# A three-step software pipeline on one core: fewer waits on TensorE and a new hand-written order of the second stage

## What is computed

```python
for i in range(DEPTH):                                   # DEPTH = 6, on x of (8, 512, 128)
    x = attn_layer(shift_tokens(x), Wqkv[i], q_scale[i], k_scale[i], Wo[i]) + x
    x = ffn_layer(shift_tokens(x), ln_g[i], ln_b[i], W1[i], b1[i], W2[i], b2[i]) + x

def attn_layer(x, Wqkv, qs, ksc, Wo):
    q, k, v = jnp.split(x @ Wqkv, 3, -1)                 # 16 heads of 64
    q, k = l2norm(q) * qs, l2norm(k) * ksc
    q = q * cos * scale + rotate_half(q) * sin * scale
    k = k * cos * inv + rotate_half(k) * sin * inv
    return local_attention(q, k, v) @ Wo                 # windows of 32, each sees itself and the one before

def ffn_layer(x, g, bln, W1, b1, W2, b2):
    xn = (x - mu) / jnp.sqrt(var + 1e-05) * g + bln
    a, gate = jnp.split(xn @ W1 + b1, 2, -1)             # 341 wide each
    return a * gelu(gate) @ W2 + b2
```

## Time and profile before

| What | Value |
|---|---|
| Median of 3 runs | 4945.61 us (4935.18 to 4952.09) |
| The profiled execution, its own time | 4938.53 us |
| Its span, first to last instruction | 4936.4 us |
| PE busy | 4103.4 us (83%), 60260 matmul records |
| DVE busy | 4056.8 us (82%) |
| POOL busy | 3516.9 us (71%) |
| ACT busy | 2979.7 us (60%) |
| Mean granted TensorE clock | 0.853 of full |

### The profile page before, as it was taken

The page is one execution under the profiler, slowest core; times in us unless marked ns, Lnnn a source line. Parts: engine busy times, 40 slices in busy tenths (PEclk is TensorE's granted clock), DMA queues, the critical chain, the costliest instruction groups (busy, mean ns, idle before and its releaser), DMA issues. The chain is left out here.

```text
span 4936.4 us, 154683 instructions
## 1 busy us (share of the span) xinstructions
PE 4103.4 (83%) x60260; PEld 2147.1 (43%) x60260; DVE 4056.8 (82%) x7132; ACT 2979.7 (60%) x4240; POOL 3516.9 (71%) x1655
## 2 busy tenths in 40 slices
PE   3666666666647999899999999899998999899995
PEld 1233223233223555455544555455554555455552
DVE  6999999999956888788878888788887888788883
ACT  5999999999953555445544555455544555455441
POOL 4999999999965676666766676567665766576661
PEclk9755555555558999999999999999999999999997
DMA  0000000000004444444553444444444444444443
GB/s 14 3 5 9 5 9 5 5 9 5 7 8 107 114 113 109 113 103 109 116 123 92 107 113 109 99 114 111 109 114 97 113 109 109 98 118 109 108 98 82
DMA packets 234267, 382.36 MB, mean 77 GB/s; under 512 B 38432, under 2 KB 63776, under 8 KB 233504
## 3 DMA queue, kind: packets, MB, share of 16 engines
q1 hardware_dynamic: 229408, 371.06, 31.9%
q10 hardware_dynamic: 4224, 2.10, 0.1%
HBM read 51.89 MB, written 18.87 MB: 14 GB/s over the span
## 5 line engine op out<-in xcount | busy, mean ns | idle before, releaser
L734 POOL TENSOR_TENSOR W<-W 128x1280 f32<-128x1280 f32 x416 | 954.9, 2319 | 141.2 <-ACT W L585 139.9
L585 ACT ACTIVATE W<-S,lam 128x512 f32<-128x512 f32 (+3 forms) x2048 | 952.0, 553 | 84.2 <-DVE lam L878 72.9
L1702 POOL TENSOR_TENSOR m<-m 128x1024 f32<-128x1024 f32 x384 | 902.6, 2362 | 68.3 <-DVE m L1810 68.2
L849 DVE BATCH_NORM_STATS2 stats<-W 128x6 f32<-128x512 f32 (+3 forms) x2048 | 832.4, 478 | 57.6 <-POOL W L734 56.5
L1708 POOL TENSOR_TENSOR sm<-sm,mx 128x1024 f32<-128x1024 f32 x192 | 451.7, 2353 | 504.7 <-DVE mx L1824 504.7
L1319 PE MATMUL pb<-xs,wg 128*128 128x512 f32 x1536 | 760.4, 630 | 52.8 <-DMA xs<-hist 38.4
L1555 ACT ACTIVATE lnn<-pb,cst 128x1024 f32<-128x1024 f32 x192 | 213.9, 1114 | 806.7 <-PE pb L1326 806.7
L1833 DVE SCALAR_TENSOR_TENSOR nf<-rn,m 128x1024 f32<-128x1024 f32 x384 | 616.7, 1637 | 93.0 <-ACT rn L1564 77.7
L1550 ACT ACTIVATE sq<-pb 128x1024 f32<-128x1024 f32 x384 | 381.9, 1021 | 491.8 <-PE pb L1319 491.8
L1698 POOL TENSOR_TENSOR sqs<-sq 128x1024 f32<-128x1024 f32 x192 | 456.9, 2379 | 225.2 <-ACT sq L1550 225.2
L1713 POOL TENSOR_TENSOR pr<-pr,rsum 128x1024 f32<-128x1024 f32 x192 | 407.4, 2122 | 292.6 <-DVE rsum L1846 290.3
(11 more groups left out here) (120 smaller groups left out, 7124.4 us busy)
## 6 DMA issues: line engine op xcount, KB each, us to landing
qkn<-nf SPq DMA_DIRECT2D x1536, 128.0 KB, 2.4
vr<-v SPq DMA_DIRECT2D x96, 768.0 KB, 5.9
vr<-v SPq DMA_DIRECT2D x96, 192.0 KB, 5.5
xr<-hist SPq DMA_DIRECT2D x48, 256.0 KB, 2.9
hist<-xo SPq DMA_DIRECT2D x48, 256.0 KB, 3.8
wg<-wqkv SPq DMA_DIRECT2D x24, 384.0 KB, 3.8
xs<-hist SPq DMA_DIRECT2D x48, 128.0 KB
vr<-v SPq DMA_DIRECT2D x96, 64.0 KB, 6.2
```

The costliest lines, as they stand in the source:

```text
L585: ins = nc.scalar.activation(W[:, p, h, c], S[:, j % 2, h, c], ACT.Abs_reciprocal_sqrt, bias=lam[:, j, i:i + 1])
L734: nc.gpsimd.tensor_tensor(W[:, p, h, :], W[:, p, h, :], W[:, p, h, :], ALU.mult).then_inc(s_wp[p], 1)
L849: ins = nc.vector.bn_stats(out=stats[:, p, h * NBLK + u, :], in_=W[:, p, h, UOFF[u]:UOFF[u] + UNIT[u]])
L1702: nc.gpsimd.tensor_tensor(m1[:, which, :, :], m1[:, which, :, :], m2[:, which, ::-1, :], ALU.add)\
```

## The change

Nothing is computed in another way. Four things differ, all in `stage2`.

1. PE's waits for inputs move out of the task functions into small functions (`weights_due` and so on), which `body` calls right ahead of the task. Waits that repeat one already passed are gone: `weights_due` stands once per group (4 and not 12 waits per step), `inputs_due` once (not twice), `normed_due` once (2 and not 8). PE's body has 35 waits for inputs where it had 50. The waits of `take` stay, with other partners.
2. PE's order and the banks in `HOLD` are new. `q3` and `k3` move from the end of body b to the start of body b + 1 (lag 1). `up1` stands ahead of `k0` and `q0`, `k0` ahead of `q0`, `weigh0` ahead of `v3`, `var` behind `turn0`, `out` ahead of both halves of `score0`, and `up0` between the halves of `weigh2`.
3. The orders of ACT, POOL, DVE and SP are new. On POOL `normalise(b, 0)` moves from the start of body b + 1 to the end of body b, behind both `add_rotated(b, 2, ...)`. On ACT `squares(b, 2, 1)` stands ahead of `squares(b, 2, 0)`, and `values(b, 2)` ahead of `inverse_norms(b, 2)`. On DVE `rotate(b, 3, 1)` comes ahead of `rotate(b, 3, 0)`, behind `scale`. On SP `load_xs` comes ahead of the second `load_projections`, and `store` takes step b - 2.
4. Three bodies are unrolled ahead of the loops, not four. DVE's `residual` gets one more wait (`s_xo` of the step before).

```diff
         HOLD = [
-            ("var", 2, 3), ("turn0", 1, 0), ("v3", 1, 2), ("weigh0", 1, 4), ("norm3", 1, 0), ("gate1", 2, 7),
-            ("gate0", 2, 2), ("score2", 1, 4), ("q0", 0, 0), ("k0", 0, 4), ("up1", 2, 3), ("turn1", 1, 6),
-            ("v0", 0, 2), ("weigh1", 1, 6), ("norm0", 0, 4), ("k1", 0, 0), ("q1", 0, 4), ("score3", 1, 6),
-            ("v1", 0, 2), ("turn2", 1, 6), ("up0", 2, 2), ("weigh2", 1, 6), ("norm1", 0, 0), ("score0", 0, 2),
-            ("out", 2, 6), ("turn3", 1, 4), ("q2", 0, 0), ("weigh3", 1, 4), ("k2", 0, 6), ("wo", 1, 3),
-            ("score1", 0, 0), ("norm2", 0, 6), ("mean", 1, 3), ("q3", 0, 4), ("v2", 0, 2), ("k3", 0, 6),
+            ("turn0", 1, 2), ("var", 2, 0), ("q3", 1, 6), ("k3", 1, 0), ("weigh0", 1, 2), ("v3", 1, 4),
+            ("norm3", 1, 0), ("gate0", 2, 6), ("gate1", 2, 3), ("score2", 1, 0), ("up1", 2, 2), ("k0", 0, 4),
+            ("q0", 0, 0), ("turn1", 1, 6), ("v0", 0, 2), ("weigh1", 1, 6), ("k1", 0, 0), ("norm0", 0, 4),
+            ("score3", 1, 2), ("v1", 0, 6), ("turn2", 1, 2), ("q1", 0, 4), ("weigh2", 1, 2), ("up0", 2, 6),
+            ("norm1", 0, 6), ("out", 2, 0), ("score0", 0, 4), ("turn3", 1, 2), ("q2", 0, 6), ("weigh3", 1, 2),
+            ("k2", 0, 0), ("wo", 1, 5), ("score1", 0, 6), ("norm2", 0, 0), ("mean", 1, 3), ("v2", 0, 4),
         ]
...
+            def due(s, value):
+                pe.wait_ge(s, value)
+                pe.sem_inc(held["pe"], 1)
+
+            def weights_due(n, g):
+                due(wg_in[g], 16 * n + 16)
+
+            def inputs_due(n):
+                due(xs_in, 32 * n + 32)
...
             def project(n, g, which, out):
-                pe.wait_ge(wg_in[g], 16 * n + 16)
-                pe.sem_inc(held["pe"], 1)
-                if g == 0:
-                    pe.wait_ge(xs_in, 32 * n + 32)
-                    pe.sem_inc(held["pe"], 1)
...
@@ PE, body(b)
+                if live(b, 2):
+                    take("up1", b)
+                    ups(b - 2, 1, bank("up1"))
+                if live(b, 0):
+                    take("k0", b)
+                    weights_due(b, 0)
+                    inputs_due(b)
+                    project(b, 0, 1, bank("k0"))
+                if live(b, 0):
+                    take("q0", b)
+                    project(b, 0, 0, bank("q0"))
...
@@ ACT, body(b)
                 if live(b, 0):
+                    squares(b, 2, 1)
+                if live(b, 0):
                     squares(b, 2, 0)
                 if live(b, 0):
-                    squares(b, 2, 1)
...
@@ POOL, end of body(b)
                 if live(b, 0):
+                    square_sums(b, 2)
+                if live(b, 0):
+                    add_rotated(b, 2, 1)
+                if live(b, 0):
                     add_rotated(b, 2, 0)
                 if live(b, 0):
-                    square_sums(b, 2)
+                    normalise(b, 0)
...
@@ DVE, residual and body(b)
             def residual(n):
+                dve.wait_ge(s_xo, at(n - 1, 0, 1))
+                dve.sem_inc(held["dve"], 1)
...
+                if live(b, 1):
+                    scale(b - 1)
+                if live(b, 0):
+                    rotate(b, 3, 1)
                 if live(b, 0):
                     rotate(b, 3, 0)
-                if live(b, 1):
-                    scale(b - 1)
-                if live(b, 0):
-                    rotate(b, 3, 1)
+                if live(b, 0):
+                    weighted(b, 0)
...
```

More of the change, by code:

```diff
@@ L1286, in _ @@
                     body(l * BATCH + k, l, k)
-            for b in range(STEPS, STEPS + 3):
+            for b in range(STEPS, STEPS + 2):
                 body(b, DEPTH, b - STEPS)
@@ L1455, in body @@
                 if live(b, 1):
-                    norms(b - 1, 3, take("norm3", b))
+                    take("v3", b)
+                    values(b - 1, 3, bank("v3"))
+                if live(b, 1):
+                    take("norm3", b)
+                    squares_due(b - 1, 3)
+                    norms(b - 1, 3, bank("norm3"))
                 if live(b, 2):
-                    gates(b - 2, 1, take("gate1", b))
+                    take("gate0", b)
+                    normed_due(b - 2)
+                    gates(b - 2, 0, bank("gate0"))
@@ L1473, in body @@
+                    probabilities_due(b - 1, 1)
+                    turn(b - 1, 1, bank("turn1"))
                 if live(b, 0):
-                    values(b, 0, take("v0", b))
+                    take("v0", b)
+                    weights_due(b, 1)
+                    values(b, 0, bank("v0"))
                 if live(b, 1):
-                    weigh(b - 1, 1, 0, take("weigh1", b))
+                    take("weigh1", b)
+                    turned_due(b - 1, 1)
+                    weigh(b - 1, 1, 0, bank("weigh1"))
@@ L1499, in body @@
                 if live(b, 0):
-                    norms(b, 1, take("norm1", b))
+                    take("norm1", b)
+                    squares_due(b, 1)
+                    norms(b, 1, bank("norm1"))
+                if live(b, 2):
+                    take("out", b)
+                    gated_due(b - 2)
+                    ffn_out(b - 2, bank("out"))
                 if live(b, 0):
-                    scores(b, 0, 0, take("score0", b))
-                if live(b, 2):
-                    ffn_out(b - 2, take("out", b))
+                    take("score0", b)
+                    rotated_due(b, 0)
+                    scores(b, 0, 0, bank("score0"))
                 if live(b, 0):
@@ L1507, in body @@
                 if live(b, 1):
[L1508 removed]
+                    take("turn3", b)
+                    probabilities_due(b - 1, 3)
+                    turn(b - 1, 3, bank("turn3"))
                 if live(b, 0):
[L1510 removed]
+                    take("q2", b)
+                    weights_due(b, 2)
+                    project(b, 2, 0, bank("q2"))
                 if live(b, 1):
[L1512 removed]
+                    take("weigh3", b)
+                    turned_due(b - 1, 3)
+                    weigh(b - 1, 3, 0, bank("weigh3"))
                 if live(b, 1):
@@ L1682, in _ @@
             act.wait_ge(cleared, 1)
-            for b in range(4):
+            for b in range(3):
                 body(b)
-            with act.Fori(4, STEPS) as b:
+            with act.Fori(3, STEPS) as b:
                 body(b)
@@ L1782, in _ @@
             pool.wait_ge(cleared, 1)
-            for b in range(4):
+            for b in range(3):
                 body(b)
-            with pool.Fori(4, STEPS) as b:
+            with pool.Fori(3, STEPS) as b:
                 body(b)
@@ L1988, in _ @@
             tables(0)
-            for b in range(4):
+            for b in range(3):
                 body(b)
-            with dve.Fori(4, BATCH) as b:
+            with dve.Fori(3, BATCH) as b:
                 body(b)
```

259 lines of the change are left out of this document (131 added, 128 removed).

## The result

| | before | after |
|---|---|---|
| Median of 4 runs | 4946.43 us (4935.18 to 4952.09) | 5087.32 us (5084.96 to 5088.42) |
| Ratio, 95% interval | | 1.0287 (1.0268 to 1.0306) |
| Profiled execution, its span | 4936.4 us | 5086.5 us |
| Mean granted clock | 0.853 | 0.844 |
| Mean ordinary step, 2140 to 4750 us, from branch to branch | 68.2 us | 71.8 us |

What follows compares the result with a forecast made beforehand. The prediction took PE to set the pace, with DVE 8 us behind. Its sum was 4938.5 + 17 (ordinary steps) - 42 (openings) = 4913 us for the profiled execution, so a 4920 us median; range 4830 to 4990.

Steps and rivals of the forecast that it cites:

- Dropped waits: On PE in ordinary steps: repeated waits gone and short waits removed by the new order, 2.2 us a step won.
- four short waits: PE's waits at `q0`, `v0`, `up0` and `out`, 1.6 us a step plus 0.16 us each; all should go.
- Three late producers: Ordinary steps: PE waits at `turn0`, `norm1` and `gate0` for results that come late, 2.65 us a step lost.
- (a): `turn0` waits for `normalise(b, 0)`, now last on POOL: PE loses 0.8 us a step.
- (b): `norm1` takes the banks of `up0` and waits for gates 0 and 1: 0.9 us a step lost.
- (c): `gate0` takes the banks of `q3` and waits for q's rotation, 0.8 us lost; `norm3` loses 0.15.
- Openings: Each layer's first step: `xs` and `qkn` waits go, `k1` loses 4.6 us to DVE's tables; five openings win 42 us.
- the first rival: The three producers in ordinary steps aren't late, so the 2.2 us are kept: 4830 us given, chance 0.27.
- code arrives late: `score0`, `turn3`, `q2` and `weigh3` in one run outpace instruction fetch: 2 us a step more, 5006 us, chance 0.20.
- the halt in `weigh3`: PE's existing halt of 1.3 us a step amid `weigh3`, no producer named, its place in the body hardly moving.
- The rival of the clock: Three new short idles on PE bring a half-clock stretch in every second step: 37 us, 4957 us, chance 0.10.

Runs made afterwards that it cites:

- e6_align: The kernel after with the wide matmuls of ten tasks split in two, 80 more PE instructions ahead of `score0`: 4848.67 us, ratio 0.9809.
- e6_again: The kernel after with the same ten tasks split, measured a second time: 4851.54 us, ratio 0.981.
- e12: The kernel before with all its repeated waits, 60 instructions added ahead of `weigh3` by splitting matmuls: 4866.91 us, ratio 0.984.
- e11: The kernel before without its 15 repeated waits, 68 instructions added ahead of `weigh3`, only 16 of them ahead of `weigh2`: 4848.25 us, ratio 0.9793.
- e9_tail: The kernel after with 60 instructions added by splitting matmuls, all behind `weigh3`: 4928.25 us, ratio 0.9958.
- e2_split: The kernel after with `out` put back between the two halves of `score0`: 5154.14 us, ratio 1.046.
- e4_before_waits: The kernel before with only its 15 repeated waits of PE dropped, orders, banks and loop edge untouched: 4947.94 us, ratio 1.0016.

## Why the prediction was wrong, and where it was right

**The terms of the sum held, as a sum.** With hardly a halt left, the change is worth 4850 - 4867 = -17 us (e6_align and e6_again against e12), with an uncertainty of some 15 us. The sum gave -26. That agrees, but it is also hardly clear of nothing, so the single terms say more:
- Dropped waits: the step put 2.2 us a step on them. Of this, 19 us / 43 = 0.4 us is due to the dropping (e12 against e11, within the noise named there), the rest to the new order, in which all four short waits are gone. That waits behind matmuls of 512 columns cost little held.
- Three late producers: (a) 0.5 us (0.6 in the prediction's list), hidden in the kernel after by the halt at the branch, (b) 0.8 in the kernel after (forecast 0.7), but only 0.5 in every second step of e6_align, (c) 0.57 (forecast 0.6). Together with 0.16 each this is 2.4 us at most, where 2.65 was taken. The mechanism and the names of the waits were right.
- Openings: the wait on `xs` is gone, and `k1` waits 5.6 us for DVE (forecast 4.6). An opening costs 8.7 us over an ordinary step in the kernel after and 7.6 in e6_align (forecast 7.1), and 15.4 in the kernel before, as a mean of four, where one window had given 16. The halts are little of this: in e12 and e11, the old order without halts, it is 13.6 and 15.1. So the term is 5 x 6.0 = 30 to 5 x 7.5 = 38 us, not 42.
- A slip: half of the 2.2 us kept gives 4945.6 - 47 - 42 = 4856, where the first rival has 4865. Nothing rests on it.

**The step that failed.** The sum has no term for code. It moved `q3` and `k3` across the loop's back edge, priced their data, and took the edge itself at nothing. The edge costs 159 us (e9_tail). The account closes with the runs: 159 us at the edge, 78 at the two borders where the old order had 4946 - 4867 = 79 at its one, and -17 for the rest, make the 141 us. The rival "code arrives late" had the right mechanism, the chance 0.20, and 5006 us, but three things were wrong in it too. First, the place. It looked at the stretch from `score0` to `weigh3` and priced 86 us more there. That stretch costs 78 us, but it had cost 79 before, so it adds about nothing. It did not look at the back edge. `q3`, `v2` and `k3` had been standing between `score1` and the branch. Before, the sequencer was held there by their waits and reached the branch 4.5 us after passing the last wait of `norm2`; now it is 1.3 us after (one step of each). Second, the halt in `weigh3` was read as part of the cost of `weigh3`, a thing the order would carry along unchanged. It is an accident of counting: it costs the kernel before those 79 us, which no row of the forecast offered as a gain. Third, the reason given, more than 500 dense instructions in a row, is not the one: e2_split broke the run up and lost 67 us, e6_align kept it whole and lost nothing there.

The rival of the clock was small, but there: the mean granted clock over 2140 to 4750 us is 0.980 before, 0.967 after and 0.991 in e6_align. Taken as full and half speed, that is 53, 87 and 23 us of the 2610, so about 34 us of the loss, near the 37 that it priced for the whole of stage 2. It is large where the halts are; no run changed the clock alone.

The Trainium skill's "Runtime: NRT & Kernel Launch", section "Instruction fetch mechanics", says that a taken branch to a target outside the loaded pages must fetch it first. By this rule the place of the edge should have been a rival of its own. The trace agrees: the branch took 0.46 us where the last code packet had ended 3.4 us before, and up to 6.66 where it ended 1.4 to 1.6 us behind one. The Trainium skill's "Advanced Engine Details and Errata", section "ISA Cache", which the prediction cited, gives the block of 256 instructions, and the halts at multiples of 256 agree. Its "Only 2 cache lines!" led me to the wrong reading that the length of a dense run decides.

**What stays open.** When the fetch of the next block begins, and why. Its packet starts 0.5 to 1.6 us after the last border was crossed in most places, but 2 to 8 us after in others. Behind the border in `weigh3` it is 6.6 us in the kernel before, 8.7 in the kernel after, 3.3 in e9_tail and 0.7 in e6_align, where `weigh3` does not halt; behind the border in `score1`, the last one ahead of the branch, it is 1.0, 4.1, 1.0 and 1.0 us. So in the kernel after a late packet behind `weigh3` is followed by a late one ahead of the branch, which fits that e6_align healed the branch by healing `weigh3`. But e9_tail healed the branch with `weigh3` halting, so that is not the whole of it, and why the last block's length changed the branch so much (107 instructions 5.05 us, 167 instructions 1.55 us) is not explained. A rival for the late starts was not tested: the same DMA engines carry the data, and in the first 3.5 us of the branch that starts at 3056.16 they were busy throughout (DMA share 1.05). Nor does the offset decide alone: 191 to 267 halted in the runs of the table, but 197 in `score1` of e4_before_waits did not, nor 202 to 212 in `weigh0`, the first run behind the branch, and `weigh2` of e6_align lost 0.6 us at 80 in its second half.

## What to carry over

In a hand-ordered loop longer than a few code blocks, look at the duration of the back edge's branch and count where the blocks' borders fall before costing any reordering: an edit that adds or drops a few instructions can move the time by more than what it was made for. Put the edge where the sequencer is held back or where much wide work is queued, not right behind a run of short instructions, and look first at borders in the last quarter of such runs and right behind them: the long halts stood there, though not every such border halts. Splitting wide matmuls shifts the borders at almost no cost, and here it made both orders some 2% faster than the kernel before, and equal to each other (4849 and 4848 us).

## What was not expected of the hardware

- The branch of a loop took 0.46 us in one order of its body and 5.05 us in another (at most 6.66 there). In the slow order it always ended 1.36 to 1.60 us after a code packet did.
- Every halt of the table stood at a multiple of 256 instructions from the loop's first, and ended 1.4 to 1.6 us (medians) after a code packet.
- 60 added instructions of TensorE made the kernel 159 us faster (e9_tail), 80 made it 238 us faster (e6_align).
- Splitting matmuls of 512 columns into 256 or 128 took no measurable time. In e6_align weight loads are busy for 1645 of 2610 us and in the kernel before for 1335, and the time of a step is not longer for it:

```profile
2140.00:4750.00 2610.00, 2497.24 (x46451) 1644.52 (x46455) 2105.95 (x2317) 1356.45 (x1393) 1776.36 (x813) 0.99 0.48 112
```
